# Layer 1 of a masked-attention stack: VectorE takes two key tiles per instruction, and the per-query rows are made on 128x16 values

## The reference

```
Wh = einsum('bnf,fo->bno', h, W)
s_i = Wh @ a[:256, 0];  s_j = Wh @ a[256:, 0]
e = leaky_relu(s_i[:, :, None] + s_j[:, None, :], 0.2)
e = where(adj > 0 or diagonal, e, -inf)
h_prime = einsum('bij,bjo->bio', softmax(e, axis=-1), Wh)
x = layernorm(x + elu(h_prime))
```

## Time and profile before

| | us |
|---|---|
| median of 3 runs | 4035.5 (4033.26 to 4039.04) |
| the profiled execution | 4037.52 |
| its span | 4035.0 |
| layer 0 ends, layer 1 begins, about | 2698 |
| one whole batch of layer 1 (span time 3008.5 to 3163.7) | 155.2 |

### The profile page before, as it was taken

One profiled execution on the slowest core, in us unless ns is written; L12 is line 12 of the kernel. 1 busy time (PEld: TensorE's weight loads), 2 busy tenths in 40 slices (PEclk: granted clock), 3 DMA queues, 4 the chain that ended last, 5 costly groups with the idle time before them and its releaser, 6 DMA issues. The chain is left out here.

```text
span 4035.0 us, 71120 instructions
## 1 busy us (share of the span) xinstructions
PE 3749.1 (93%) x25476; PEld 1764.5 (44%) x25476; DVE 3096.8 (77%) x4053; ACT 2503.3 (62%) x3554; POOL 2038.1 (51%) x1068
## 2 busy tenths in 40 slices
PE   6999999999999999999999999952998998899998
PEld 1333323333323332332333333321776777777777
DVE  6676777677577677677767757858889889899897
ACT  3565656566666566566656566631676776776777
POOL 1776777677677677677767768842011011011010
PEclk9999999999999999999999999976999999999999
DMA  5000000001000000000000100023110110111101
GB/s 213 1 32 12 22 33 12 12 14 41 12 12 32 22 12 33 12 22 33 12 12 13 42 12 12 22 96 139 32 53 26 49 53 22 53 40 35 32 24 39
DMA packets 106437, 141.08 MB, mean 35 GB/s; under 512 B 3793, under 2 KB 87633, under 8 KB 104017
## 3 DMA queue, kind: packets, MB, share of 16 engines
q1 hardware_dynamic: 104816, 135.80, 10.1%
q10 hardware_dynamic: 1248, 0.40, 0.1%
HBM read 102.63 MB, written 33.55 MB: 34 GB/s over the span
## 5 line engine op out<-in xcount | busy, mean ns | idle before, releaser
L368 ACT ACTIVATE probs<-probs 128x1024 f32<-128x1024 f32 x1024 | 1080.4, 1055 | 945.9 <-DVE probs L621 915.4
L621 DVE SCALAR_TENSOR_TENSOR probs<-sc_ps,clip_hi 128x1024 f32<-128x1024 f32 x1024 | 1203.2, 1216 | 572.8 <-PE sc_ps L446 568.9
L267 POOL TENSOR_TENSOR psums<-probs 128x1024 f32<-128x1024 f32 x512 | 1246.6, 2457 | 163.4 <-ACT probs L368 163.4
L1075 PE MATMUL out_ps<-wh,e 128*128 128x257 f32 x4096 | 964.6, 389 | 166.0 <-DVE e L1217 159.9
L446 PE MATMUL sc_ps<-q_cols,k_cols 64*128 64x512 f32 x4096 | 1022.3, 617 | 25.1 <-DVE probs L621 12.6
L462 PE MATMUL ctx_ps<-probs,v_rows 128*32 128x512 f32 x8192 | 977.3, 595 | 1.2 <-DVE seg_ctx L544 1.2
L1075 PEld LDWEIGHTS out_ps<-wh,e 128*128 128x128 f32 x4096 | 778.1, 193 | 326.8 <-DVE e L1217 120.6
L278 POOL TENSOR_TENSOR ctx_t<-ctx_t,seg_ctx 128x1024 f32<-128x1024 f32 x224 | 534.2, 2385 | 604.5 <-DVE seg_ctx L544 604.4
L446 PEld LDWEIGHTS sc_ps<-q_cols,k_cols 64*128 64x128 f32 x4096 | 353.1, 186 | 698.0 <-issue 575.4
L904 POOL TENSOR_TENSOR rstd<-var_eps,minus_half 128x4 f32<-128x4 f32 x32 | 68.4, 2138 | 1069.9 <-DVE var_eps L1177 1069.9
L462 PEld LDWEIGHTS ctx_ps<-probs,v_rows 128*32 128x32 f32 x8192 | 255.8, 110 | 597.8 <-issue 550.2
(11 more groups left out here) (85 smaller groups left out, 2393.8 us busy)
## 6 DMA issues: line engine op xcount, KB each, us to landing
x_cols<-in_xT SPq DMA_DIRECT2D x8, 2048.0 KB, 10.2
probs<-in_adjT SPq DMA_DIRECT2D x16, 1024.0 KB, 8.4
x_rows<-in_x SPq DMA_DIRECT2D x32, 512.0 KB, 4.8
x<-res SPq DMA_DIRECT2D x32, 512.0 KB, 3.3
x_in<-x SPq DMA_DIRECT2D x8, 2048.0 KB, 10.9
x_res<-x SPq DMA_DIRECT2D x32, 512.0 KB, 4.6
out<-h SPq DMA_DIRECT2D x32, 512.0 KB, 3.2
e<-in_adjT SPq DMA_DIRECT2D x8, 1024.0 KB, 7.9
```

The costliest lines, as they stand in the source:

```text
L267: pool.tensor_tensor(psums[:, q % 2, pair, :], probs[:, (SJ * q) % RING, pair, :], probs[:, (SJ * q + 1) % RING, pair, :], ALU.add).then_i ...
L368: act.activation(probs[:, n % RING, pair, :], probs[:, n % RING, pair, :], ACT.Exp, scale=DH ** -0.5).then_inc(s_exp, 1)
L621: dve.scalar_tensor_tensor(out=probs[:, n % RING, pair, :], in0=sc_ps[:, p, :, :], scalar=-LIM, in1=clip_hi[:, j, c * CW:(c + 1) * CW][:, ...
L1075: last = pe.matmul(out_ps[:, bank(c, t), 0:F + 1], e[:, n % ERING, t * P:(t + 1) * P], wh[:, p, j, 1:F + 2], start=(j == 0), stop=(j == JB ...
```

## The change

- `larger_sides(n)` and `mask_two(n)` take tiles n and n + 1 in one instruction of 128x1024. VectorE's stream has, in even steps n only: `larger_sides(n + 2)`, then `mask_two(n)`. The ring `e_low` grows from 4 tiles to 8; `e` stays at 8. ScalarE's stream keeps AHEAD = 3.
- s_i is made as one more column of Wh (258 columns in place of 257), and the four `s_row` uses on TensorE and their copies on ScalarE go.
- The rows are made on 128x16 values: SyncE stores the s_i column to DRAM and loads it back as 128x16 (`s_c`), and spreads the reduced maxima out of one partition to 128x16 (`m_c`). VectorE does its four row operations on those, all in step 54. SyncE stores the two rows to DRAM (16 KB) and loads each back to all 128 partitions (1 MB each) into `best` and `low`. `sides` of the next batch's step 0 waits for these two loads.

The core of the diff:

```diff
-    LRING = 4
+    LRING = 8
-    TU, WU, SU = KB * NC, JB, NC
-    USES = TU + WU + SU
+    TU, WU = KB * NC, JB
+    USES = TU + WU
-    ROWS_AT = (53, 55, 57, 59)
+    ROWS_AT = 54
 ...
+            def spread_own(b):
+                sp.wait_ge(s_prepread, count(b, USES, 2 + TU + WU))
+                    sp.dma_start(s_d[0].rearrange("(j p) -> p j", p=P), wh[:, b[1] % 2, :, 0]).then_inc(s_sout, 16)
+                sp.wait_ge(s_sout, count(b, 16, 16))
+                sp.dma_start(s_c[:, :], s_d[0].rearrange("(p j) -> p j", p=P)).then_inc(s_sin, 16)
+            def make_rows(b):
+                p = b[1] % 2
+                sp.wait_ge(s_all, count(b, 1, 1))
+                sp.dma_start(m_c[:, :], low[0:1, p, :].rearrange("o (q j) -> o q j", j=RJ)).then_inc(s_m, 16)
+                sp.wait_ge(s_rows, count(b, 4, 4))
+                sp.dma_start(rows_d.rearrange("r (p j) -> p r j", p=P), rows_c[:, :, :]).then_inc(s_rout, 16)
+                sp.wait_ge(s_rout, count(b, 16, 16))
+                sp.dma_start(best[:, p, :], rows_d[0].partition_broadcast(P)).then_inc(s_rin, 16)
+                sp.dma_start(low[:, p, :], rows_d[1].partition_broadcast(P)).then_inc(s_rin, 16)
 ...
+                    if c == 2 and more:
+                        spread_own(following(b))
+                    if c == NC - 1 and more:
+                        make_rows(following(b))
 ...
                 if n == 0:
-                    act.wait_ge(s_rows, count(b, 4, 4))
+                    act.wait_ge(s_rin, count(b, 32, 32))
 ...
                 if k == 0:
-                    dve.wait_ge(s_prepread, count(b, USES, 2 + USES))
-                    dve.wait_ge(s_all, count(b, 1, 1))
-                    dve.tensor_tensor(low[:, p, :], low[:, p, :], s_row[:, :], ALU.add).then_inc(s_rows, 1)
+                    dve.wait_ge(s_sin, count(b, 16, 16))
+                    dve.wait_ge(s_m, count(b, 16, 16))
+                    dve.tensor_tensor(m_c[:, :], m_c[:, :], s_c[:, :], ALU.add).then_inc(s_rows, 1)
 ...
+            def larger_sides(b, n):
+                tiles = e[:, n % ERING:n % ERING + 2, :]
+                dve.wait_ge(s_lo, count(b, STEPS, n + 2))
+                dve.wait_ge(s_hi, count(b, STEPS, n + 2))
+                dve.tensor_tensor(tiles, tiles, e_low[:, n % LRING:n % LRING + 2, :], ALU.max).then_inc(s_max, 2)
+            def mask_two(b, n):
+                dve.wait_ge(s_max, count(b, STEPS, LRING + n + 2))
+                dve.scalar_tensor_tensor(out=tiles, in0=mask[:, j:j + 2, c * CW:(c + 1) * CW], scalar=0.0,
+                                         in1=tiles, op0=ALU.max, op1=ALU.min).then_inc(s_e, 2)
 ...
-                        if n + 1 < STEPS:
-                            larger_side(b, n + 1)
-                        elif more:
-                            larger_side(following(b), 0)
-                        dve.wait_ge(s_max, count(b, STEPS, LRING + n + 1))
-                        dve.scalar_tensor_tensor(out=tile, in0=mask[:, j, c * CW:(c + 1) * CW], scalar=0.0,
-                                                 in1=tile, op0=ALU.max, op1=ALU.min).then_inc(s_e, 1)
+                        if j % 2 == 0:
+                            if n + 2 < STEPS:
+                                larger_sides(b, n + 2)
+                            elif more:
+                                larger_sides(following(b), 0)
+                            mask_two(b, n)
```

More of the change, by code:

```diff
@@ L681, in _, with layer1 @@
             run(dve, prologue, chunk, tail)
-def layer1(nc, x1, adjT, W, a, out):
+def layer1(nc, x1, adjT, W, a, s_d, rows_d, out):
     B, N, F = x1.shape
@@ L692, in layer1 @@
     AHEAD = 3
-    LRING = 4
+    LRING = 8
     OUT_BANKS = 6
-    TU, WU, SU = KB * NC, JB, NC
-    USES = TU + WU + SU
-    uses_at = [1 + u for u in range(TU)] + [10 + 27 * j // JB for j in range(JB)] \
-        + [37 + 2 * c for c in range(NC)]
+    TU, WU = KB * NC, JB
+    USES = TU + WU
+    RJ = N // P
+    uses_at = [1 + u for u in range(TU)] + [10 + 27 * j // JB for j in range(JB)]
     TAKEN = 4
@@ L863, in prologue @@
                 load_x((0, 1))
+                spread_own((0, 0))
+                make_rows((0, 0))
             def steps(b, chunks, prev, more):
@@ L1040, in prepare @@
                     for k in range(KB):
-                        last = pe.matmul(prep_ps[:, u % 2, 0:F + 1], x_cols[:, k, j * P:(j + 1) * P],
+                        last = pe.matmul(prep_ps[:, u % 2, 0:F + 2], x_cols[:, k, j * P:(j + 1) * P],
                                          w_ext[:, k, :], start=(k == 0), stop=(k == KB - 1))
[L1043 to L1048, removed]
                 last.then_inc(s_prep, 1)
@@ L1092, in _ @@
             for k in range(KB):
-                for i, (row, dst) in enumerate(((a1_r, wa1[:, k:k + 1]), (a2_r, w_ext[:, k, 0:1]))):
-                    dve.tensor_tensor_reduce(out=trash[:, 2 * k + i, :], in0=w_ext[:, k, 1:F + 1], in1=row[:, :],
+                for i, (row, dst) in enumerate(((a1_r, w_ext[:, k, 0:1]), (a2_r, w_ext[:, k, 1:2]))):
+                    dve.tensor_tensor_reduce(out=trash[:, 2 * k + i, :], in0=w_ext[:, k, 2:F + 2], in1=row[:, :],
                                              scale=1.0, scalar=0.0, op0=ALU.mult, op1=ALU.add,
                                              accum_out=dst).then_inc(s_wa, 1)
[L1097 to L1101, removed]
             def mask_piece(i):
@@ L1237, in steps @@
                                 fifths(following(b))
-                            if n in ROWS_AT:
-                                row_operation(following(b), ROWS_AT.index(n))
+                            if n == ROWS_AT:
+                                for k in range(4):
+                                    row_operation(following(b), k)
             def tail(b):
@@ L1256, in build @@
     layer0(nc, x, xT, adjT, wqT, wkT, wvT, woT, bq, bk, bv, bo, gamma, beta, x1)
-    layer1(nc, x1, adjT, W, a, out)
+    s_d = nc.dram_tensor("s_own", (1, x.shape[1]), F32, kind="Internal").ap()
+    rows_d = nc.dram_tensor("rows", (2, x.shape[1]), F32, kind="Internal").ap()
+    layer1(nc, x1, adjT, W, a, s_d, rows_d, out)
 def kernel(x, adj, L0_gnn_Wq, L0_gnn_bq, L0_gnn_Wk, L0_gnn_bk, L0_gnn_Wv, L0_gnn_bv, L0_gnn_Wo, L0_gnn_bo,
```

59 lines of the change are left out of this document (28 added, 31 removed).

## The result

The changed kernel takes 4119.9 us (median of 4 runs, 4118.1 to 4122.1) against 4035.9 us for the kernel before on the same chip: a ratio of 1.0208, with a 95% interval of 1.0190 to 1.0226. It is slower by 84 us. The forecast was 4112, in a range of 4060 to 4165.

What follows compares the result with a forecast made beforehand. VectorE was taken to set the time in chunks 1, 2 and 3, TensorE in the last batch. Batches with preparation +52, last batch +17, start +7: 76 us on the 4035.5 median gives 4112, range 4060 to 4165.

Steps and rivals of the forecast that it cites:

- VectorE's work falls by 12.5 us a batch: VectorE's passes and row operations: pairs save 4.5 us a batch; row operations go from 8.8 to 0.8 us.
- rival 3: VectorE's passes: a pair isn't cheaper, through the two-run mask operand or longer tiles; 4128 to 4145 us, chance 0.08.
- A lead of two steps is lost: VectorE's step n needs ScalarE's exponentials n + 2 and n + 3, not n + 1; chunks without preparation take 32.7 us.
- Chunk 1, +3.3: Chunk 1 of a batch, 46.4 us before: work 45.4, idle 1.85 + 2.45, sum 49.7, so 3.3 us longer.
- Chunk 2, +3.5: Chunk 2 of a batch, 39.6 us before: 43.1 with waits and a pass held beside GpSimd's reduction, 3.5 us longer.
- chunk 0, +0.4: The next batch's chunk 0, 34.5 us before: 32.7 plus `take` copies and the first maximum, 34.9, so 0.4 us longer.
- Chunk 3, +0.3 with D = 10: Chunk 3, 34.6 us before: row operations, transfers of 10 us, then 12.1 us to the next reciprocals: 35.0, 0.3 longer.
- D: Time from the end of the row operations until the rows are in SBUF, one store and two loads: taken as 10 us.
- The repeated row (rival 2): Loads of the rows: repeating one 8 KB row 128 times is slow, transfers take 20 us; 4191 us, chance 0.12.
- The last batch and the start: Last batch: three chunks of 32.7 against 27.4, +16, last chunk +1, together +17; before the first product: +7 us.
- VectorE's work decides (rival 1): Whole kernel: ScalarE runs ahead, VectorE's idle time stays near 12 us a batch; 50 us faster, 3986, chance 0.10.
- half the waits (rival 4): VectorE's waits for ScalarE: 1.2 us a chunk less over 31 chunks, 37 us; 4074 us, chance 0.20.

Runs made afterwards that it cites:

- Pairs alone: Kernel before with only VectorE's two passes changed to pairs, `e_low` at four tiles, row operations 2048 wide: 4154.9 us, 1.0298.
- The kernel with the lead back: Changed kernel with AHEAD = 5 in place of 3, nothing else different: 4004.6 us, 0.9925 of the kernel before.
- rows only: Changed kernel with VectorE's two passes put back to single tiles, `e_low` at four tiles, AHEAD 3: 3990.3 us, 0.9889 of the kernel before.
- single tiles and AHEAD 5: Changed kernel with both passes tile by tile, `e_low` at four tiles, and AHEAD = 5 in place of 3: 3987.6 us, 0.9880 of the kernel before.

## Why the prediction was right, step by step

- **VectorE's work falls by 12.5 us a batch.** Right: 12.3. Both parts were right too, 4.35 and 8.3 for 4.5 and 8.0, by the two kernels with one part each. A paired larger side is followed after 1.14 us (4011.56 to 4012.70), and a paired mask pass after 1.14 as well (3126.72, the next pass at 3127.86), so the two-run mask operand costs nothing more and rival 3 is out. Pairs alone have 512 passes fewer and 34.8 us less work: 0.068 us for each pass saved. The Trainium skill (VectorE: DVE Perf Modes, "The TRN2 errata") gives a duration whose fixed part is 0.157 us; an estimate from it makes the saving 80 us. The durations agree with it and the saving doesn't, because each pass starts before the one ahead of it has ended; the measurement decides for 0.07.
- **A lead of two steps is lost.** Right, and shown from both sides: given back it brings 115 us, taken from the kernel before it costs 133. The waits stand where the forecast put them, to 0.3 us (4.03, 2.12, 2.48 and 1.07 for 3.85, 2.2, 2.45 and 1.15), and a chunk bound by that loop takes 33.0 us for 32.7.
- **Chunk 1, +3.3.** The step that was sized too small: +4.3 in the typical batch. Two thirds of the missing 1.0 us are idle time: 50.70 less 45.74 is 4.96 against 4.3, with 2.00 behind the reciprocals, 0.30 behind `exp_h`, which I had let a maximum cover wholly, and 2.48 behind `offset`. The rest is work, 45.74 against 45.4; the maxima come to 2.26 to 2.32 us each. That makes 7 of the 9 us by which the sum of chunk 1 was under-called. The other 2 lie in two batches, the third and the fifth, whose chunk 1 is long in both kernels (47.8 and 49.3 before, 55.4 and 52.1 after). In the third after the change ScalarE's copy waited for a preparation product of TensorE, and VectorE behind it (ScalarE's row, then VectorE's):

```profile
3195.91 0.39 ACT L978 ACTIVATE wh<-prep_ps 128x258 f32<-128x258 f32 x1 [4.72 <-PE prep_ps L1066]
```

```profile
3200.91 1.22 DVE L1217 TENSOR_TENSOR e<-e,e_low 128x1024 f32<-128x1024 f32 x1 [4.97 <-ACT e L990]
```

  The preparation is late because TensorE's clock is low there. TensorE's row ahead of it:

```profile
3188.28 6.72 PE L1094 MATMUL out_ps<-wh,e 128*128 128x257 f32 x16 [2.83 <-ACT h L997]
```

  These sixteen records, the products of two steps, take 6.72 us; the same ones of the second batch (from 3022.65) take 3.63. The granted clock is 0.55 over the first, nearly all of it at the lower level of 1.2 GHz, and 1.00 over the second. TensorE had stood still for 2.83 us before. In the fifth batch it stood still for 2.61 us, the clock stayed at 1.00 and the sixteen took 3.73. Before the change the clock fell in the fifth batch instead (5.42 us for the sixteen, behind 2.89 us of idle time) and not in the third (3.73, behind 3.05). So which of these chunks the clock hits differs from kernel to kernel. The standing still does not: every kernel here has it, 2.6 to 3.4 us, at the start of chunk 1 of the third and the fifth batch, and in no other batch over 2 us there. These are the two places where the program's loop over pairs of batches (`Fori`) jumps back to its start. The queues that carry instructions move 6 packets between 3177 and 3190 us, and 6 in the 110 us behind. That the streams wait for code is my reading; no run changed the loop.
- **Chunk 2, +3.5, chunk 0, +0.4.** +3.8 and +0.5 on average. Chunk 0 is split: 35.0 in four batches, 36.4 in two, where the forecast had 34.9 for all.
- **Chunk 3, +0.3 with D = 10.** -0.2 on average. D is smaller. The last row operation, the three issues and the first exponential behind it:

```profile
3129.50 0.17 DVE L1158 SCALAR_TENSOR_TENSOR rows_c<-s_c,m_c 128x16 f32<-128x16 f32 x1
3129.70 0.36 SPq L869 DMA_DIRECT2D rows<-rows_c  x1
3131.26 0.33 SPq L871 DMA_DIRECT2D best<-rows  x1
3131.64 0.43 SPq L872 DMA_DIRECT2D low<-rows  x1
3138.47 0.72 ACT L987 ACTIVATE e_low<-low,s_fifth 128x512 f32<-128x512 f32 x1 [5.67 <-DVE e L1217]
```

  From 3129.67 to 3138.47 are 8.8 us. What releases the exponential is the landing of `low` (3131.64 and the 6.7 below, 3138.34). The row names a larger side that ends at 3138.45, but that pass takes the tiles of steps 62 and 63, which this exponential doesn't need; in the other six batches the same wait is put down to the transfer (36.6 us in six). `norm_h` follows at 3139.71, just as `offset`, for which it waits, has ended (3139.64). So D stands at the point below which the loop itself is later, and this chunk takes 33.5 where the forecast named 33.6 for that case. The kernel with the lead back shows D alone: its last row operation ends at 3102.82 and its exponential starts at 3111.56, 8.7 us. The store had landed after 1.5 us, not 2.2.
- **The repeated row (rival 2).** Out. The two loads of 1 MB landed 4.5 and 6.7 us after their issue:

```profile
best<-rows SPq DMA_DIRECT2D x7, 1024.0 KB, 4.5
low<-rows SPq DMA_DIRECT2D x7, 1024.0 KB, 6.7
s_own<-wh SPq DMA_DIRECT2D x7, 8.0 KB, 10.7
s_c<-s_own SPq DMA_DIRECT2D x7, 8.0 KB, 1.9
m_c<-low SPq DMA_DIRECT2D x7, 8.0 KB, 2.0
rows<-rows_c SPq DMA_DIRECT2D x7, 16.0 KB, 1.5
```

  From the first issue (3131.26) to the second's landing (3131.64 + 6.7) are 7.1 us for 2 MB, 296 GB/s with all that is fixed in it. Repeating one 8 KB row costs nothing to be seen; the 134 GB/s of the earlier trace rows belong to packets of about 1 KB (356 of them, 0.33 MB). The 103 to 207 GB/s of the Trainium skill (DMA: Bandwidth & Descriptors, "Latency and other measured facts"), which the prediction set against this part, are measured there for rows 512 KiB to 8 MiB apart, and its lock-step mechanism is called an inference; a row that is repeated is another case, and the slow rate did not come.
- **The last batch and the start.** +17.9 for +17, with the last chunk +1.8 and not +1; +5.5 for +7, again the shorter D.
- **VectorE's work decides (rival 1), half the waits (rival 4).** Both are out. Rival 1 set its own limit: under 12.5 us of added idle time a batch. In the batch shown VectorE's idle time rose from 12.1 to 32.7 us, by 20.6. Even with AHEAD 5 the time is 4004.6, not the 3986 of rival 1's account. Rival 4 wanted waits 1.2 us a chunk shorter; they stand at full size (4.03, 2.12, 2.48 and 1.07).

## What to carry to other kernels

A pass over two tiles at steps n and n + 1 needs its second tile two steps earlier than two single passes did, so the merge is even only if the producer's program gets that lead too; it is a number in the code (here AHEAD), and it belongs to the width. Before merging, ask what a saved instruction is worth from start to start, not by its duration: here 0.07 us, which no version tried with pairs earned back, while the row operations on 128x16 values brought 45 us alone. When work falls and time rises, cut the trace at the same event in both kernels and look at the stretch where no engine is full.

The version to keep is rows only: 3990.3 us, 0.9889 [0.9872, 0.9905] of the kernel before, or 3987.6, 0.9880 [0.9863, 0.9896], with AHEAD 5; the two can't be told apart.

## What the runs showed of the hardware

- A pass of VectorE that meets GpSimd's reduction is held, at either width: in all these kernels it ends 4.1 to 5.7 us behind the reduction's start. The changed kernel's chunk 2, GpSimd's row and VectorE's:

```profile
3108.77 6.12 POOL L928 PARTITION_ALL_REDUCE low<-best  x1 [5.85 <-issue]
```

```profile
3108.85 4.59 DVE L1217 TENSOR_TENSOR e<-e,e_low 128x1024 f32<-128x1024 f32 x1 [1.07 <-ACT e L990]
```

  The pass of 1024 ends 4.67 us behind that start; before, the one of 512 ended 4.49 us behind it (3089.53 to 3094.02). The Trainium skill (SBUF — State Buffer, "SBUF: two separate sides") calls the port pair that the two engines share an exclusive lock for the whole of an instruction. The trace agrees that a pass is blocked, but it is free again before the reduction's shown 6.1 us are over (a span of GpSimd in the profile is rough). With single tiles and AHEAD 5 chunk 2 ends as the reduction begins (3084.38, 3083.91), so the held pass moves to chunk 3, which has room for it (3084.66, 3.73 us): chunk 2 falls from 39.6 to 35.1 and chunk 3 rises from 27.8 to 29.0. Chunk 0 rises by 2.5 in the same kernel, which eats much of that. Over seven batches VectorE's `elu` waits for `exp_h` there for 24.7 us, against 4.7 in rows only, and ScalarE's exponentials wait for TensorE's products in the ring of eight for 18.5 us, against none. That is the cost that I had expected of the long lead.
- The 8 KB store in 4-byte pieces landed after 10.7 us, five times the 1.9 to 2.0 us of an 8 KB transfer in longer pieces. Here it had time.
- In every kernel one or two of the seven batches have a chunk 1 that is 1 to 5 us longer than the others: the third, the fifth or both, where the loop jumps back and TensorE stands still for about 3 us. In the third batch of the changed kernel and the fifth of the one before, the lower clock behind it adds to that.
